# Mean of x1 summed from g in pass 1, and the pooling stages of two sequences run side by side

## The reference

```
x1 = x + 0.5 * ffn(LN(x))         # s = x Win + bin (64 wide), h = relu(s W1 + b1), g = h W2 + b2, out = g Wout + bout
mq = LN(x1) Wq + bq ; mk = LN(x1) Wk + bk
q_w = softmax over the sequence of (mq Wqa + bqa) / 8      ; pooled_q = sum_s q_w * mq   (per head)
k_w = softmax over the sequence of ((mk*pooled_q) Wka + bka) / 8 ; pooled_k = sum_s k_w * mk * pooled_q
x2 = x1 + (pooled_k * mq) Wt + bt + mq
out = x2 + 0.5 * ffn(LN(x2))
```

## The kernel before

| stage | sequence 0 | sequence 1 |
|---|---|---|
| 1 | q pooling (pbq) | |
| 2 | k score maxima (p2a) | q pooling (pbq) |
| 3 | k pooling (p2b) | k score maxima (p2a) |
| 4 | | k pooling (p2b) |

## Time and profile before

### The profile page before, as it was taken

The page is one execution under the profiler, slowest core; times in us unless marked ns, Lnnn a source line. Parts: engine busy times, 40 slices in busy tenths (PEclk is TensorE's granted clock), DMA queues, the critical chain, the costliest instruction groups (busy, mean ns, idle before and its releaser), DMA issues.

```text
span 2510.7 us, 22296 instructions; the slowest of 8 cores (2494.8 to 2510.7 us)
## 1 busy us (share of the span) xinstructions
PE 1742.1 (69%) x6246; PEld 577.6 (23%) x6340; DVE 1008.8 (40%) x1892; ACT 528.2 (21%) x662; POOL 38.4 (2%) x78
## 2 busy tenths in 40 slices
PE   0558888788888888888923445665877784778785
PEld 0212222222232222222300101111222220222221
DVE  0123333333333333333335445555544443444443
ACT  0232222222222222221000000000233231223232
POOL 0000000000000000000000000000000000000000
PEclk9868998898999999899955557755898896989896
DMA  9212222322122222211133444433142415242321
GB/s 145 67 51 68 85 85 68 84 85 84 42 67 80 85 85 85 68 52 52 52 103 105 121 138 136 137 85 93 51 130 72 138 39 127 87 143 72 105 71 67
DMA packets 174773, 220.28 MB, mean 88 GB/s; under 512 B 6176, under 2 KB 138528, under 8 KB 174016
## 3 DMA queue, kind: packets, MB, share of 16 engines
q1 hardware_dynamic: 126784, 160.15, 20.3%
q10 hardware_dynamic: 44448, 46.70, 6.1%
q0 software_dynamic: 3424, 12.00, 3.1%
HBM read 146.38 MB, written 84.44 MB: 92 GB/s over the span
## 4 chain that ended last, share of the span: by engine, by line
PE 60%; DVE 16%; DMA 9%; issue 7%; ACT 6%; ACTq 1%; DVEq 1%; SPq 0%; POOLq 0%
PE pb L1063 9%; PE pb L805 9%; PE pb L773 9%; DVE h_bf L606 5%; PE pb L522 4%; PE pb L510 4%; DMA esc_s<-escq_d 4%; DVE x_s L1154 3%; PE pb L942 3%; PE pb L491 3%; DVE x_bf L691 3%; ACT big_s L717 2%; PE pb L1129 2%; PE pb L725 2%; PE pb L810 2%
## 5 line engine op out<-in xcount | busy, mean ns | idle before, releaser
L601 PE MATMUL pb<-eb_s,esel_s 16*128 16x512 bf16 x256 | 137.8, 562 | 227.6 <-DVE eb_s L595 169.7
L517 ACT ACTIVATE h_bf<-pb,b1f_s,w1f_s 128x512 bf16<-128x512 f32 x256 | 198.7, 776 | 444.0 <-PE pb L510 444.0
L805 PE MATMUL pb<-x_bf,wk_s 128*128 128x512 bf16 x994 | 241.7, 380 | 1.6
L773 PE MATMUL pb<-x_bf,wq_s 128*128 128x512 bf16 x992 | 238.8, 380 | 3.4 <-issue 2.5
L816 DVE CAST ptk_s<-pb 128x512 bf16<-128x512 f32 x128 | 88.6, 692 | 270.6 <-PE pb L810 270.6
L535 PE MATMUL pb<-g_bf,wout_s 64*128 64x512 bf16 x256 | 128.9, 525 | 97.5 <-DVE x_s L1154 33.1
L522 PE MATMUL pb<-h_bf,w2bd_s 128*64 128x512 bf16 x256 | 108.8, 425 | 85.0 <-ACT h_bf L517 85.0
L1081 DVE TENSOR_TENSOR x_s<-pb,rf_s 128x512 f32<-128x512 f32 x128 | 88.5, 692 | 177.1 <-PE pb L1068 174.1
L784 DVE CAST ptq_s<-pb 128x512 bf16<-128x512 f32 x128 | 86.8, 690 | 129.5 <-PE pb L778 127.0
L1154 DVE SCALAR_TENSOR_TENSOR x_s<-pb,bout_s,x_bf 128x512 f32<-128x512 f32 x128 | 96.1, 751 | 105.1 <-PE pb L535 92.5
L1063 PE MATMUL pb<-ptq_s,wt_s 128*128 128x512 bf16 x496 | 123.0, 389 | 21.1 <-DMA ptq_s<-ptq_d 15.8
(11 more groups left out here) (146 smaller groups left out, 1760.4 us busy)
## 6 DMA issues: line engine op xcount, KB each, us to landing
x_s<-xT SPq DMA_DIRECT2D x16, 2048.0 KB, 12.7
out<-x_s SPq DMA_DIRECT2D x16, 2048.0 KB, 8.3
x_d<-x_bf ACTq DMA_DIRECT2D x16, 1024.0 KB
ptq_d<-ptq_s SPq DMA_DIRECT2D x16, 1024.0 KB, 4.4
ptk_d<-ptk_s SPq DMA_DIRECT2D x16, 1024.0 KB, 4.4
x_bf<-x_d SPq DMA_DIRECT2D x16, 1024.0 KB, 14.0
ptq_s<-ptq_d SPq DMA_DIRECT2D x12, 1024.0 KB, 8.5
ptq_s<-ptk_d SPq DMA_DIRECT2D x8, 1024.0 KB, 5.9
```

Source lines behind the costliest of these rows:

```text
L517: S_op(lambda e, c=c, eb=eb: e.activation(out=h_bf[:, c % 2, :], in_=pb[eb][:], func=AF.Relu, bias=b1f_s[:, c:c + 1], scale=w1f_s[:, c:c + ...
L601: T_op(lambda e, c=c, ebk=ebk: e.matmul(pb[ebk][:], esel_s[:, c, :], eb_s[:, par, :], start=True, stop=True), ["ebbf%d" % par, "esel"], [" ...
L773: ins = [e.matmul(pb[wb][:], wq_s[:, kc, j * 128:(j + 1) * 128], x1_bf[:, par, kc, :], start=(kc == 0), stop=False) for kc in range(NCH)]
L805: ins = [e.matmul(pb[wb][:], wk_s[:, kc, j * 128:(j + 1) * 128], x1_bf[:, par, kc, :], start=(kc == 0), stop=False) for kc in range(NCH)]
```

## The change

Two independent edits. First, sums2 no longer sums x1 over its eight chunks. Since x1 = x + Wout-product of g + bout2, the negated mean of x1 is the negated mean of x (mrow_s, already there), plus a product of g_bf with the column sums of wout (cswout_bf, 64x1), plus a constant (s2b_s). So two matmuls of 512 columns take the place of eight, and the constant is added where ln_stats before only copied the row (tensor_scalar in place of tensor_copy). The column sums and the constant are made once in the setup. Second, the middle has three stages in place of four: q pooling of both sequences, k maxima of both, k pooling of both, and in p2_buf the two sequences swap their buffers for even tiles.

```diff
--- before.py
+++ after.py
@@ -249,6 +249,9 @@
         bqa_s = sbt("bqa_s", [H, 1]); bka_s = sbt("bka_s", [H, 1])
         bqa2_s = sbt("bqa2_s", [H, 1]); bka2_s = sbt("bka2_s", [H, 2])
         b2_s = sbt("b2_s", [FM, 1]); b2_bf = sbt("b2_bf", [FM, 1], BF16)
+        cswout_f = sbt("cswout_f", [FM, 1]); cswout_bf = sbt("cswout_bf", [FM, 1], BF16)
+        sb128_f = sbt("sb128_f", [128, 1]); sb128_bf = sbt("sb128_bf", [128, 1], BF16)
+        s2b_s = sbt("s2b_s", [1, 1])
         eps_s = sbt("eps_s", [1, 1]); zero_s = sbt("zero_s", [128, 1])
 
         x_s = sbt("x_s", [128, 2, NCH, T])
@@ -426,14 +429,37 @@
                 scalar1=bout_s[:, j:j + 1], scalar2=0.5,
                 op0=ALU.add, op1=ALU.mult) for j in range(NCH)],
              ["pb_sc", "bout"], ["bout2"], "bout2")
+        V_op(lambda e: e.reduce_sum(cswout_f[:], wout_s[:], axis=AX.X),
+             ["wout"], ["cswf"], "cswf")
+        V_op(lambda e: e.tensor_scalar(out=cswout_bf[:], in0=cswout_f[:],
+                                       scalar1=-1.0 / D, scalar2=None,
+                                       op0=ALU.mult),
+             ["cswf"], ["cswout"], "cswout")
+        V_op(lambda e: e.reduce_sum(sb128_f[:], bout2_s[:], axis=AX.X),
+             ["bout2"], ["sb128f"], "sb128f")
+        V_op(lambda e: e.tensor_copy(sb128_bf[:], sb128_f[:]),
+             ["sb128f"], ["sb128b"], "sb128b")
+        T_op(lambda e: e.matmul(pb[PB_S2][0:1, 0:1], ones_s[:, 1:2],
+                                sb128_bf[:], start=True, stop=True),
+             ["sb128b", "ones"], ["pb%d" % PB_S2], "s2bmm")
+        S_op(lambda e: e.activation(out=s2b_s[:], in_=pb[PB_S2][0:1, 0:1],
+                                    func=AF.Copy, bias=0.0, scale=1.0),
+             ["pb%d" % PB_S2], ["s2b"], "s2bcp")
 
         def ln_stats(pba, pbb, par, mslot, stat_row, t0, tag,
-                     onchip_r64=False, store=True):
+                     onchip_r64=False, store=True, madd=None):
             key = "stt%d" % par
 
-            V_op(lambda e: e.tensor_copy(stat_s[0:1, par, 0, :],
-                                         pb[pba][0:1, :]),
-                 ["pb%d" % pba], [key + "_m"], tag + "_cm")
+            if madd is None:
+                V_op(lambda e: e.tensor_copy(stat_s[0:1, par, 0, :],
+                                             pb[pba][0:1, :]),
+                     ["pb%d" % pba], [key + "_m"], tag + "_cm")
+            else:
+                madd_ap, madd_key = madd
+                V_op(lambda e: e.tensor_scalar(
+                        out=stat_s[0:1, par, 0, :], in0=pb[pba][0:1, :],
+                        scalar1=madd_ap, scalar2=None, op0=ALU.add),
+                     ["pb%d" % pba, madd_key], [key + "_m"], tag + "_cm")
             V_op(lambda e: e.tensor_mul(stat_s[0:1, par, 1, :],
                                         stat_s[0:1, par, 0, :],
                                         stat_s[0:1, par, 0, :]),
@@ -720,19 +746,21 @@
                  x1keys, [sqk, "wqT"], "p1_sq1")
 
             def sums2(e):
-                ins = []
-                for c in range(NCH):
-                    ins.append(e.matmul(pb[PB_S1][0:1, :], ones_s[:, 1:2],
-                                        x1_bf[:, par, c, :],
-                                        start=(c == 0), stop=(c == NCH - 1)))
+                ins = [e.matmul(pb[PB_S1][0:1, :], cswout_bf[:], g_bf[:],
+                                start=True, stop=False),
+                       e.matmul(pb[PB_S1][0:1, :], onerow_s[0:1, 0:1],
+                                mrow_s[0:1, par, :],
+                                start=False, stop=True)]
                 for c in range(NCH):
                     ins.append(e.matmul(pb[PB_S2][0:1, :], ones_s[:, 2:3],
                                         sq_ap[:, c, :],
                                         start=(c == 0), stop=(c == NCH - 1)))
                 return ins
-            T_op(sums2, x1keys + [sqk, "ones"],
+            T_op(sums2, x1keys + [sqk, "ones", "g", "cswout", "onerow",
+                                  "mrow%d" % par],
                  ["pb%d" % PB_S1, "pb%d" % PB_S2], "p1_sums2")
-            ln_stats(PB_S1, PB_S2, par, 2 + par, 1, t0, "p1ln2_%d_%d" % (si, ti))
+            ln_stats(PB_S1, PB_S2, par, 2 + par, 1, t0, "p1ln2_%d_%d" % (si, ti),
+                     madd=(s2b_s[0:1, 0:1], "s2b"))
             bcast_r(1, t0, "r16_%d" % par, r16_s[:, par, :], H, "p1_r16")
 
         BANKS = [(PB_W0, "pb_w0"), (PB_W1, "pb_w1"),
@@ -918,9 +946,9 @@
                  ["pb_sc", "bka2a"], ["bka2"], "p1_bka2")
 
         def p2_buf(par, ti):
-            primary = ((ptq_s, ["ptq_%d" % j for j in range(NCH)])
+            primary = ((ptk_s, ["ptk_%d" % j for j in range(NCH)])
                        if par == 0
-                       else (ptk_s, ["ptk_%d" % j for j in range(NCH)]))
+                       else (ptq_s, ["ptq_%d" % j for j in range(NCH)]))
             return tile_buf(primary, par, ti)
 
         def p2_load(si, ti, tag):
@@ -1191,40 +1219,35 @@
                 for c in range(NCH):
                     p1_D3_j(si, ti, c)
                 p1_D3sp(si, ti)
-            eb2_final(0, 0, bqa2_s[:], "bqa2", "p1eb2_0")
-            eb2_final(1, 0, bqa2_s[:], "bqa2", "p1eb2_1")
+            for si in seqs:
+                eb2_final(si, 0, bqa2_s[:], "bqa2", "p1eb2_%d" % si)
             for ti in range(cfg.ntile + 1):
-                if ti < cfg.ntile:
-                    pbq_load(0, ti)
-                if ti > 0:
-                    pbq_chain(0, ti - 1)
-            p1_fin(0)
-            p2_init(0)
+                for si in seqs:
+                    if ti < cfg.ntile:
+                        pbq_load(si, ti)
+                    if ti > 0:
+                        pbq_chain(si, ti - 1)
+            for si in seqs:
+                p1_fin(si)
+            for si in seqs:
+                p2_init(si)
             for ti in range(cfg.ntile + 1):
-                if ti < cfg.ntile:
-                    pbq_load(1, ti)
-                    p2_load(0, ti, "p2a_0_%d" % ti)
-                if ti > 0:
-                    pbq_chain(1, ti - 1)
-                    p2a_chain(0, ti - 1)
-            p1_fin(1)
-            p2_init(1)
-            eb2_final(0, 1, bka2_s[:, 0:1], "bka2", "p2eb2_0")
+                for si in seqs:
+                    if ti < cfg.ntile:
+                        p2_load(si, ti, "p2a_%d_%d" % (si, ti))
+                    if ti > 0:
+                        p2a_chain(si, ti - 1)
+            for si in seqs:
+                eb2_final(si, 1, bka2_s[:, si:si + 1], "bka2",
+                          "p2eb2_%d" % si)
             for ti in range(cfg.ntile + 1):
-                if ti < cfg.ntile:
-                    p2_load(1, ti, "p2a_1_%d" % ti)
-                    p2_load(0, ti, "p2b_0_%d" % ti)
-                if ti > 0:
-                    p2a_chain(1, ti - 1)
-                    p2b_chain(0, ti - 1)
-            eb2_final(1, 1, bka2_s[:, 1:2], "bka2", "p2eb2_1")
-            p2_fin(0)
-            for ti in range(cfg.ntile + 1):
-                if ti < cfg.ntile:
-                    p2_load(1, ti, "p2b_1_%d" % ti)
-                if ti > 0:
-                    p2b_chain(1, ti - 1)
-            p2_fin(1)
+                for si in seqs:
+                    if ti < cfg.ntile:
+                        p2_load(si, ti, "p2b_%d_%d" % (si, ti))
+                    if ti > 0:
+                        p2b_chain(si, ti - 1)
+            for si in seqs:
+                p2_fin(si)
             for sidx, si in enumerate(seqs):
                 p3_wtscale(si, reload=(sidx > 0))
                 p3_load(si, 0)
```

## The result

| | before | after |
|---|---|---|
| median | 2519.42 us (10 runs) | 2503.05 us (11 runs) |
| ratio | | 0.9942, 95% interval 0.9929 to 0.9955 |
| the profiled execution | 2512.27 | 2507.84 |
| spans of the 8 cores | 2494.8 to 2510.7 | 2484.6 to 2506.3 |

Some executions run in a slower state of the chip; the medians are over all runs, the ratio is of the others alone. So the change makes the kernel some 15 us faster (11 to 18, from the ratio). The prediction said 47 us, 2470 us, range 2450 to 2498.

A forecast was written before the change was run, and what follows sets the result against it. TensorE was taken to bound the first part, the latency of its chains the middle. Gains of 41 us (middle) and 8 (mean sum) less 1.7 (setup) made 47, from 2517.45 to 2470 us, range 2450 to 2498.

The forecast's parts named there:

- Setup: Start of the kernel: added reductions, scale and cast on VectorE ahead of the first cast of x lose 1.7 us.
- the dear kind: First-part tiles whose clock rises late and sums1 starts slow: 14.2 us, about five of 15, each to gain 2.3.
- a tile of the good kind: First-part tile with early clock rise: sums2 7 slow and 3 fast matmuls, 6.1 us with pause; 11.2 against 10.9 in all.
- the 5.1 us of sums1: First part: sums1 expected to start slow after the pause and take 5.1 us in most tiles, as at 691.06.
- rival (b): First part: the clock takes the saving back or more, -26 to 0 us; total 2478 to 2504; chance 0.26.
- rival (a): First part: removed matmuls count in full, clock pattern unhurt, gain 20 to 36 us; total 2450; chance 0.13.
- Stage A: Middle, q pooling of both sequences: 16 chains of 8.1 us plus three waits of 6.8, ending at 1423.7 us.
- three exposed waits: q pooling in the middle: VectorE stands 6.8 us for sequence 0's scores at tiles 3, 5 and 7.
- Stage B: Middle, k maxima of both sequences: 18.2 us, then three rounds of 19.5 (58.5), ending at 1500.4 us.
- Rival (c): Middle: simultaneous loads on both queues slow scores to 8.6 us and rounds to 23.5; gain 3, total 2508; chance 0.14.
- waits for r16: Middle, first two stages: waits for the r16 load priced at nothing; seeing them would show the prediction wrong.
- Stage C: Middle, k pooling of both sequences: first chain 13.4 us, then 15 of 12.24, ending at 1697.4 us.

The follow-up runs named there:

- e2: The kernel before with only the second edit, the new order of the middle and swapped buffers; median 2494.8 us, ratio 0.9878.
- e3: The changed kernel without the key wqT shared by both halves of big_s, so each load waits for its own half; median 2464.2 us, ratio 0.9753.
- e9: e3 with r16 in two buffers for each sequence in place of one; middle 427.1 us, median 2466.8 us, ratio 0.9793 to the kernel before.
- e5: The changed kernel with sums2 in the free banks PB_E0 and PB_E1, so sums1 need not wait for VectorE; round 65.58 us, ratio 0.9669.
- e4: The changed kernel with six more matmuls, result unread, in the pause behind sums2; round 68.10 us, median 2474.2 us, ratio 0.9791.
- e11: The changed kernel plus e5's banks, e3's keys, two r16 buffers, chunked x1 square, stage C's next head and scores earlier, x's cast later; 2384.5 us, ratio 0.9458.
- e12: e11 with the cast and first square of x cut into eight chunks between the groups of Wk; round 96.38 us, median 2794.7 us, ratio 1.1094.
- e6: The kernel before with six more unread matmuls in the pause behind sums2; round 69.21 us, median 2509.6 us, ratio 0.9977.
- e13: The changed kernel with even-tile loads in stage B waiting until the odd load before them on the queue landed; middle 470.8 us, ratio 0.9904.

## Why the prediction was wrong

**Setup.** +3.0 against 1.7 us. e2, without the first edit, has its first store at 141.5 us, so the loss belongs to that edit; which of its operations costs more than said was not looked into.

**First part.** Right: the two kinds of tile in the kernel before (on core 6 five rounds of 14 at 71.4 to 71.8 us, the others 68.2 to 68.8), sums1 slow in nearly all tiles behind the change (118 of 120), and the way the sum was made. The share of the dear kind was read from one core: over the eight it is 50 of 120, not a third.

The step that failed: "a tile of the good kind would be 7 slow and 3 fast matmuls, 3.6 us". In 88 of 120 tiles all ten are slow, in the others all but the last one or two: 4.6 us where all are, and on the mean of all tiles 7.0 with the pause where 6.1 was put. Beside it the 5.1 us of sums1, taken from the tile at 691.06, hold for 56 tiles only; in 62 it takes 6.2. Together a tile of after pays 12.7 us on the mean where 11.2 and 11.9 were put. With the measured means and shares the prediction's sum gives 15 x (12.3 - 12.7), a loss of some 6 us in place of a gain of 8; the rounds lost 3.

This is rival (b). The rule quoted against rival (a), that the warm-up is a budget of time and not a number of matmuls (the Trainium skill, TensorE: Matmul & The Clock Gate, Part 1), agrees with L749 to L755 as far as it denies a fixed number: the clock rose behind some seven at 762.60 and not within ten here. That it is a fixed time they don't show either. I cited the rule and then took the seven of one tile as a count myself. Why the seven of the earlier trace rows were enough at 762.60, and ten are not now, is open.

**Stage A.** Right: three exposed waits, 20.8 us by e3 against 20.4 said, and on every core of after three waits of 6.4 to 7.3 us. The stage takes 169.1 us on the mean of the cores, 169.3 was said. Core 4 is 3.5 over, about half of it since its first chain began 20.9 us behind the last store (19.3 said).

**Stage B.** The mis-sized term is the round: 69.6 us for the three on the mean (63.8 to 74.8) against 58.5. "Each time the odd load of sequence 0 (5.7 us, as behind it in A)": it took 8.8 on the mean. The earlier trace rows had the rate at which two queues load, and I used it only as a lower bound. Rival (c) put a round at 23.5; the mean was 23.2. Its other half, slow scores in every round of A, did not come. The waits for r16, priced at nothing and named as a sign of being wrong, are there, VectorE in stage B (core 4):

```profile
1459.81 0.68 DVE L578 TENSOR_TENSOR esc_s<-pb,r_s 16x512 f32<-16x512 f32 x1 [5.73 <-DMA r_s<-stat_d]
```

TensorE stood 5.05 us behind this one. Whether they cost time while the odd loads pace the round is not shown; once the key was gone they cost 6 us of the middle (e9).

**Stage C and the end.** 12.24 us a chain, as said. From the end of stage B to the third part the kernel takes 213.4 us on the mean against 210.6 said; the 2.8 us are not in the chains. The swapped buffers cost nothing (third part 760.5 against 760.1).

**The base.** The largest error that is not in the working. The prediction took 41 us off the middle of core 6, 497.6 us. That was the longest of the eight; the mean is 486.9. Of the 25 us missing in the middle, 10.7 are this, 11 are the rounds of stage B and 3 lie behind stage B. That the total of 2503 us falls into the range of rival (b), 2478 to 2504, is luck: (b) kept the middle's 41 us, of which 16 came. A view of one core's stages would have to be taken on all cores before terms of 10 us are made of it.

## What to carry to other kernels

Matmuls taken out between two pauses of TensorE bought nothing here, since the engine then started slow behind each: take the pause out (another PSUM bank, e5: 4.4 us a round), or fill it (e4: 1.8). Count such stretches in all tiles and on all cores: the one tile looked at first stood for half of them. Before reordering loops, list what each load must wait for by its keys: one name shared by two halves of a buffer cost 38 us here, more than the whole reordering gave. And where an operation is moved on an in-order engine, look at what then stands behind it on that engine, as e11 and e12 show.

## What the runs showed of the hardware

Six matmuls more in a pause made a round of the kernel before 1.0 us shorter on six of its cores (69.75 to 68.8), and one of the changed kernel 1.8.

Behind a pause of 2.50 to 2.57 us TensorE ran at either level in the kernel before: in 70 of 120 tiles sums1 ran on at 0.216 us a matmul (2.4 GHz), in those whose clock had risen by the eleventh matmul of sums2; in 50, whose clock had risen later, about eight matmuls of sums1 took 0.43 us. In after (2.56 to 2.92 us of pause, ten matmuls ahead of it, at most the last two fast) 118 of 120 tiles were slow again. With 0.1 to 1.6 us of pause (e4, e6) all 240 were fast.

Of two 1 MB loads issued 1.8 us apart by SP the first landed after 8.4 us on the mean (second and third round of stage B, 5.7 to 11.3), and after 6.6 where the second waited for it (second round of e13). The Trainium skill (DMA: Bandwidth & Descriptors, Two DMAs through the same engine are not ordered) says that descriptors within one queue of one DMA engine start in order but are pipelined. The landing times agree with such an overlap, though ScalarE's loads under way beside them may have a part.
